# Four value groups at a time, and scores by key from the first maximum on, in a Perceiver's cross attentions

## The chip, the cores and the metric

The kernel runs as one program on one core of a Trainium2 chip. The metric is the device time of an execution in microseconds, lower is better; of several runs the median counts.

## The reference

Four layers work on a stream x of 256 tokens of width 256. Each layer has a cross attention from the stream to a context of 4,096 tokens, then an attention-like step among the 256 tokens and a feed-forward step. The change touches the cross attentions. Those of layers 2 and 3 are plain:

```python
qh = (q @ Wq.T + bq).reshape(B, Sq, H, HD).transpose(0, 2, 1, 3) / sqrt(HD)
kh = (k @ Wk.T + bk).reshape(B, Sk, H, HD).transpose(0, 2, 1, 3)
vh = (v @ Wv.T + bv).reshape(B, Sk, H, HD).transpose(0, 2, 1, 3)
scores = jnp.einsum('bhqd,bhkd->bhqk', qh, kh)
attn = jax.nn.softmax(scores, axis=-1)
ctx = jnp.einsum('bhqk,bhkd->bhqd', attn, vh)
```

with H = 16 heads of width 16, 256 queries (the normalised stream) and 4,096 keys. Layer 1 has a mask on the keys of each query; layer 0 has a mask too and multiplies the softmax by a given weight per query and key.

## The kernel before

The keys and values of all four layers are projected first. After that each layer runs `cross`, which puts three stages into one block: `queries`, `attend` and `project_out`. In `attend` every engine has its instruction list written out by a loop over the heads, and the engines meet at semaphores alone.

A head's scores are computed twice. **By query** (`by_queries`, L861): a chunk is 512 keys for 128 queries, one matmul into one bank of PSUM, and 16 chunks make a head. The vector engine only takes the maximum of each row of a chunk (L1070; with a mask L1066), and from 16 such columns the maximum of each query (`row_max`, L1075). GpSimd splits that maximum into three bf16 parts in four short steps (`split`, L1159 to L1162), the tensor engine turns it (`turn_max`, L931) and the scalar engine places it as three more rows of the queries' operand (`place_max`, L986), which signals max_set. **By key** (`by_keys`, L878; with a mask also L881): four key tiles of 128 keys by 256 queries, two banks, the maximum already subtracted by the three rows; 8 such groups make a head. The scalar engine exponentiates a group of 128 x 1024 (L1046) into one of eight buffers `prob`, and the tensor engine multiplies it with the values (`values`, L905, four matmuls of 32 columns each, side by side in the array), adding up in one bank. Values lag four groups behind. After a head's last group the scalar engine copies the sums (`read_sums`, L991), the tensor engine folds them (`fold`, L940) and the vector engine normalises (L1095, L1097).

The order of the tensor engine, and with it the steps of the scalar and the vector engine, is a string per head: C is a chunk by query, K a group by key, V two groups of values, T the turn of the next head's maximum, F the fold of the head before. In `PLAIN_ORDER` each head takes 16 C, 8 K and 4 V, and its C's run 24 chunks ahead: head h reduces the last 8 chunks of head h+1 and the first 8 of head h+2, so the turn T of head h+1 needs the eighth C of head h. The scalar engine places the maximum of head h+1 after the sixth group of head h (`TURN_AT`) and copies the sums of head h-1 after the fourth (`SUM_AT`).

Three limits tie the queues together. C and F share a ring of three banks: `ring_bank` waits until the reduction three uses ago is done. K has two pairs of banks: a group waits for the exponential two groups before. The exponential of group n waits until the values of group n-8 are done.

Ahead of the heads stands an opening of `FIRST` passes. A pass is two chunks into one of three pairs of banks, and the vector engine reduces 128 x 1024 at once. With `FIRST` = 12 the opening covers 24 chunks, that is head 0 and half of head 1; the maximum of head 0 is turned after pass 10 (`n == SC // 2 + 2`). In attention 1 GpSimd also prepares three groups of the mask (L1199, L1201) before it splits the first maximum.

```python
ORDER = WEIGHTED_ORDER if weighted else MASKED_ORDER if by_query else PLAIN_ORDER
i = slots.next()
if i >= RING:
    pe.wait_ge(S("s_read"), i - RING + 1)
```

Of the kernel before, what the change touches and what calls it, by code (L numbers as in the profile page):

```python
# [37 lines left out]
NGROUP = KT // GROUP  # L38
# [29 lines left out]

WEIGHTED_ORDER = "WK CCK C V C T C WK CCK C V F C WKK CCC V C KK W CCC V".replace(" ", "")
MASKED_ORDER = "CCK CCK CCK CVV CCK KCCKF CKCT KCCC VV".replace(" ", "")  # L70
PLAIN_ORDER = "CCKCKCCV CCKCKCV CKCCT KF CKCCKC VV".replace(" ", "")


class Sems:
# [695 lines left out]
def attend(c, l, by_query, weighted, ctx, asked, load_next):  # L770
# [3 lines left out]
    SC = QT * NCHUNK  # L774
    LAG = 2 if weighted else 4
    NP = 2 * LAG
    AHEAD = 32 if weighted else 24
    FIRST = AHEAD // 2
    ORDER = WEIGHTED_ORDER if weighted else MASKED_ORDER if by_query else PLAIN_ORDER
    SUM_AT, TURN_AT = (1, 1) if weighted else (2, 5) if by_query else (3, 5)  # L780
    SHIELD = (2, 5, 7) if l == SHIELDED else ()
    SHARED = (0, 2, 4, 6) if weighted else ()
    RING = 3
    ops, kop, qop, vraw = c.ops, c.ops.kop, c.qop, c.ops.vraw
    S = Sems(nc, ctx, f"att{l}")
    sb = lambda name, shape, dt: ctx.enter_context(nc.sbuf_tensor(f"{name}_a{l}", shape, dt))
# [22 lines left out]
    first_banks = [pair(0), pair(3), pair(5)]  # L809
    last_first = [max(n for n in range(FIRST) if n % 3 == r) for r in range(3)]  # L810
    st_order = sorted((1, 2), key=lambda r: last_first[r])
# [29 lines left out]
    def _(pe):  # L841
# [101 lines left out]

        for n in range(FIRST):
            if 2 * n % SC == 0:
                loaded(2 * n // SC)
            if n >= 3:
                pe.wait_ge(S("first_read"), n - 2)
            for i in range(2):
                ins = by_queries(first_banks[n % 3][:, i * CHUNK:(i + 1) * CHUNK], 2 * n + i)  # L950
            ins.then_inc(S("first_psum"), 1)
            if n == SC // 2 + 2:
                turn_max(0)

        for h in range(H):
            at, g, n = SC * h + AHEAD, 0, NGROUP * h - LAG
            for step in ORDER:
                if step == "C":
                    if at < SC * H:
                        if at % SC == 0:  # L960
                            loaded(at // SC)
                        by_queries(ring_bank(), at).then_inc(S("s_psum"), 1)
                    at += 1
                elif step == "K":
                    by_keys(h, g)
                    g += 1
                elif step == "V":
                    if n >= 0:
                        two_values(n)
                    n += 2  # L970
                elif step == "T" and h + 1 < H:
                    turn_max(h + 1)
                elif step == "F" and h > 0:
                    fold(h - 1)
# [6 lines left out]
    @stage.scalar  # L981
    def _(act):
        def place_max(h):

            act.wait_ge(S("max_turned"), h + 1)
            act.activation(qop[R_MAX:R_MASK, h, :], turn_out[R_MAX:R_MASK, :], ACT.Copy).then_inc(S("max_set"), 1)  # L986

        def read_sums(h):

            act.wait_ge(S("pv_psum"), NGROUP * (h + 1))  # L990
            act.activation(acc[:, h % 2, :], sums_out, ACT.Copy).then_inc(S("sums_read"), 1)  # L991

        if asked is None:
            act.activation(warm[:, :], c.ones[:, 0:1], ACT.Exp).then_inc(S("table"), 1)
        def sum_part(h, t, j, lowered, at):

            if h >= 4 and t == 0 and j == own[0]:
                act.wait_ge(S("gathered"), h - 3)
            act.activation(lowered, lowered, ACT.Exp, scale=-1.0, bias=best[:, h % 2, at:at + 1],  # L999
                           accum_out=part[:, h % 4, t, own.index(j):own.index(j) + 1]).then_inc(S("summed"), 1)  # L1000

        def find_scale(h):

            act.wait_ge(S("max_found"), h + 1)
            least = best[:, h % 2, :].rearrange("p (t j two) -> p t j two", t=QT, two=2)
            for t in range(QT):
                act.activation(scale[:, h % 4, t, :], least[:, t, :, 0 if h < 2 else 1], ACT.Exp, scale=-1.0,
                               bias=nmax[:, h % 2, t:t + 1]).then_inc(S("scaled"), 1)

        if weighted:  # L1010
            for n in range(FIRST):
                h, chunk = 2 * n // SC, 2 * n % SC
                act.wait_ge(S("first_read"), n + 1)
                sum_part(h, chunk // NCHUNK, chunk % NCHUNK + 1, used[:, n % NP, CHUNK:2 * CHUNK], chunk)
                if n == SC // 2 + 2:
                    find_scale(0)
                    place_max(0)
        else:
            place_max(0)
        slots, slot_of = Count(), {}  # L1020
        for h in range(H):
            at, g = SC * h + AHEAD, 0
            for step in ORDER:
                if step == "C":
                    last = at - 1
                    if last in slot_of and last % NCHUNK in own:
                        act.wait_ge(S("s_read"), slot_of[last] + 1)
                        hh, chunk = last // SC, last % SC
                        sum_part(hh, chunk // NCHUNK, chunk % NCHUNK, below[:, last // 2 % 2, :], chunk)
                    if at < SC * H:  # L1030
                        slot_of[at] = slots.next()
                    at += 1
                if step == "F" and h > 0:
                    slots.next()
                if step != "K":
                    continue
                n = NGROUP * h + g
                act.wait_ge(S("st_psum"), n + 1)
                if n >= NP:
                    act.wait_ge(S("pv_psum"), n - NP + 1)  # L1040
                if g in SHIELD:
                    act.activation(prob[:, n % NP, :], st_bank(n), ACT.Relu, scale=-1.0).then_inc(S("bounded"), 1)
                    act.wait_ge(S("bounded"), shields(n) + 1)
                    act.activation(prob[:, n % NP, :], prob[:, n % NP, :], ACT.Exp, scale=-1.0).then_inc(S("exp_done"), 1)  # L1044
                else:
                    act.activation(prob[:, n % NP, :], st_bank(n), ACT.Exp).then_inc(S("exp_done"), 1)  # L1046
                if g == SUM_AT and h > 0:
                    read_sums(h - 1)
                if g == SUM_AT and weighted and h + 1 < H:
                    find_scale(h + 1)  # L1050
                if g == TURN_AT and h + 1 < H:
                    place_max(h + 1)
                g += 1
        read_sums(H - 1)

    @stage.vector
    def _(dve):
# [45 lines left out]
        for n in range(FIRST):  # L1103
            h, chunk = 2 * n // SC, 2 * n % SC
# [9 lines left out]
                row_max(h)  # L1114
        dve.wait_ge(S("first_read"), FIRST)
        for h in range(H):
            at = SC * h + AHEAD
            for step in ORDER:
                if step == "C":
                    if at < SC * H:  # L1120
                        k = slots.next()
# [1639 lines left out]
```

## Time and profile before

| | us |
|---|---|
| median of three runs | 1492.37 |
| lowest and highest run | 1487.21, 1492.59 |
| the profiled execution | 1488.9 |
| its span, first to last instruction | 1487.5 |
| tensor engine, matmuls busy | 1356.0 (91% of the span) |
| vector engine busy | 1005.1 (68%) |
| scalar engine busy | 859.9 (58%) |
| GpSimd busy | 568.7 (38%) |
| mean granted clock of the tensor engine | 0.963 of full |

The heads of attention 1 lie from about 605 us on, those of attention 2 from 953 to 1153, those of attention 3 from 1242 to 1442. In a timeline a row is a run of like instructions on one engine: its start and length in microseconds, the engine, the line in the kernel, what it writes and reads, how many there are, and in brackets how long the engine was idle before and what ended that. The length of a matmul row reaches to the end of its last result, so rows overlap by the pipeline's depth, and costs are read from start to start. The matmuls of the values are recorded twice each (a row of x16 is two groups). PE is the tensor engine, DVE the vector engine, ACT the scalar engine, POOL GpSimd.

### The profile page before, as it was taken

The page shows a single profiled execution, that of the slowest core. Times are in us where ns is not written, and L with a number is a line of the kernel's source. Part 1 is how long each engine was busy: PE and PEld are TensorE (multiplying, and loading weights), DVE is VectorE, ACT ScalarE, POOL GpSimd, SP SyncE. Part 2 cuts the span into 40 slices and gives each one's busy share as a digit, 9 for nine tenths or more (in the row PEclk, how much of TensorE's full clock was granted, in tenths as well). Part 3 has the DMA queues.
Part 4 walks back from the last instruction along what each step waited for, and adds up shares of the span by engine and source line. Part 5 has one row for each costly group of instructions (what it writes and reads, how often), then busy time and mean ns, then how long its engine had stood idle before and what let it go on. Part 6 is the DMA issues. An engine that isn't in the chain of part 4 may idle for free. (4 is left out here: it accounts for less than half of the span.)

```text
span 1487.5 us, 28822 instructions
## 1 busy us (share of the span) xinstructions
PE 1356.0 (91%) x10423; PEld 802.3 (54%) x10496; DVE 1005.1 (68%) x2324; ACT 859.9 (58%) x1326; POOL 568.7 (38%) x686
## 2 busy tenths in 40 slices
PE   8999798999999988799999788699999896999987
PEld 3765656355555456355555554255555582555555
DVE  4445485999999734778787143588885337888832
ACT  5143141899999731388888552167777302777762
POOL 4565252688989920655555340111110001111100
PEclk9999999899999998899999999799999997999999
DMA  8877997246547053266655195257776711677700
GB/s 274 286 266 250 246 256 261 47 65 87 75 69 161 2 81 48 57 93 92 85 82 146 34 212 201 80 79 104 103 112 196 111 18 46 97 108 104 152 2 8
DMA packets 126008, 178.30 MB, mean 120 GB/s; under 512 B 14733, under 2 KB 106021, under 8 KB 116646
## 3 DMA queue, kind: packets, MB, share of 16 engines
q1 hardware_dynamic: 111898, 161.04, 52.9%
q10 hardware_dynamic: 13968, 15.41, 3.4%
q8 instruction: 84, 1.38, 0.4%
q14 instruction: 58, 0.48, 0.1%
HBM read 132.58 MB, written 43.78 MB: 119 GB/s over the span
## 5 line engine op out<-in xcount | busy, mean ns | idle before, releaser
L1046 ACT ACTIVATE prob_a<-ps 128x1024 f32<-128x1024 f32 x464 | 456.6, 1020 | 143.5 <-PE ps L878 95.4
L861 PE MATMUL ps<-kop,qop 116*128 116x512 bf16 x1024 | 345.4, 401 | 34.8 <-DMA qop<-qparts 21.8
L1070 DVE TENSOR_REDUCE best_a<-ps 128x1 f32<-128x512 f32 (+1 forms) x488 | 318.4, 709 | 49.4 <-PE ps L861 49.0
L878 PE MATMUL ps<-qop,kop 116*128 116x256 bf16 x2048 | 333.9, 274 | 7.7 <-ACT prob_a L1046 3.1
L878 PEld LDWEIGHTS ps<-qop,kop 116*128 116x128 bf16 x2048 | 193.8, 98 | 124.7 <-ACT prob_a L1046 21.9
L1066 DVE CUSTOM_DVE_ANT_0 dump_a<-ps,neg_q 128x512 bf16<-128x512 f32 (+1 forms) x244 | 165.9, 715 | 44.3 <-PE ps L861 42.2
L905 PE MATMUL ps<-prob_a,vop_a 128*32 128x256 f32 x3072 | 191.7, 383 | 3.1 <-POOL prob_a L1210 2.2
L861 PEld LDWEIGHTS ps<-kop,qop 116*128 116x128 bf16 x1024 | 95.2, 103 | 160.3 <-issue 64.3
L1180 POOL TENSOR_TENSOR used_a<-prob_a,gT 128x1024 f32<-128x1024 f32 x64 | 154.4, 2414 | 22.1 <-DVE used_a L1083 17.0
L1159 POOL CAST mpart_a<-nmax_a 128x2 bf16<-128x2 f32 x64 | 26.3, 411 | 348.1 <-DVE nmax_a L1075 348.1
L1210 POOL TENSOR_TENSOR prob_a<-prob_a,neg_k 128x1024 f32<-128x1024 f32 x48 | 102.5, 2135 | 92.8 <-ACT prob_a L1044 86.3
L905 PEld LDWEIGHTS ps<-prob_a,vop_a 128*32 128x32 f32 x3072 | 87.2, 109 | 82.6 <-issue 34.9
L503 PE MATMUL ps<-wv,ctxT 128*128 128x256 f32 x512 | 117.3, 392 | 14.4 <-DVE vst L648 14.4
L492 PE MATMUL ps<-ctxT,wk 128*128 128x512 f32 x256 | 112.6, 599 | 5.9 <-DMA wk<-in_wk 5.8
L503 PEld LDWEIGHTS ps<-wv,ctxT 128*128 128x128 f32 x512 | 100.5, 197 | 32.2 <-DVE vst L648 16.0
L538 ACT ACTIVATE kp<-ps,bk 128x512 bf16<-128x512 f32 x64 | 43.8, 686 | 127.8 <-PE ps L492 107.8
L1083 DVE SCALAR_TENSOR_TENSOR used_a<-prob_a,gT 128x1024 f32<-128x1024 f32 x64 | 95.5, 1492 | 9.0 <-ACT prob_a L1046 9.0
L668 POOL TENSOR_TENSOR kp<-rest,kp 128x512 bf16<-128x512 f32 x64 | 74.7, 1171 | 60.9 <-ACT kp L543 60.8
L211 POOL TENSOR_TENSOR rstd<-var,minus_half 128x2 f32<-128x2 f32 x11 | 7.8, 710 | 223.5 <-DVE var L201 215.6
L648 DVE TENSOR_TENSOR vst<-ps,bv 128x256 f32<-128x256 f32 x128 | 53.0, 423 | 59.4 <-PE ps L503 50.8
L881 PE MATMUL ps<-neg_k,identb 128*128 128x512 bf16 x225 | 86.2, 383 | 0.0
L999 ACT ACTIVATE below_a<-below_a,best_a 128x512 f32<-128x512 f32 x112 | 80.3, 717 | 9.2 <-DVE best_a L1062 8.6
(333 smaller groups left out, 1768.0 us busy)
## 6 DMA issues: line engine op xcount, KB each, us to landing
kop<-kparts SPq DMA_DIRECT2D x448, 128.0 KB, 5.2
kparts<-kp SPq DMA_DIRECT2D x64, 384.0 KB, 4.7
vals<-vst SPq DMA_DIRECT2D x16, 1024.0 KB, 5.2
vraw<-vals SPq DMA_DIRECT2D x64, 256.0 KB, 6.6
e_w<-in_e_w SPq DMA_DIRECT2D x4, 2048.0 KB, 10.8
z_w<-in_z_w SPq DMA_DIRECT2D x24, 256.0 KB, 7.0
ctxT<-in_ctxT SPq DMA_DIRECT2D x8, 512.0 KB, 8.0
raw<-in_mask ACTq DMA_DIRECT2D x16, 256.0 KB, 5.3
```

Of the source, the lines that this page charges most:

```text
L492: ins = pe.matmul(c.ps[:, K_BANKS[u % 4], :], wk[:, ct, mt * P:(mt + 1) * P], ctxT[:, ct, j * CHUNK:(j + 1) * CHUNK], start=(ct == 0), sto ...
L503: ins = pe.matmul(c.ps[:, V_BANKS[v % 4], 0:D], ctxT[:, ct, k * P:(k + 1) * P], wv[:, ct, :], start=(ct == 0), stop=(ct == CT - 1))
L861: return pe.matmul(out, qop[0:R_ALL, h, t * P:(t + 1) * P], kop[0:R_ALL, h % UNROLL, j * CHUNK:(j + 1) * CHUNK], start=True, stop=True)
L878: ins = pe.matmul(st_bank(n)[:, j * NT:(j + 1) * NT], kop[0:R_ALL, h % UNROLL, k * P:(k + 1) * P], qop[0:R_ALL, h, :], start=(j % 2 == 0), ...
L881: ins = pe.matmul(st_bank(n)[:, (j - 1) * NT:(j + 1) * NT], c.identb[:, :], c.neg_k[:, k - 1:k + 1, :], start=False, stop=True)
L905: ins = pe.matmul(sums_out[32 * j:32 * j + 32, :], vop[:, h % 2, g * GROUP + j, :], used[:, n % NP, j * NT:(j + 1) * NT], start=(g == 0 an ...
L1046: act.activation(prob[:, n % NP, :], st_bank(n), ACT.Exp).then_inc(S("exp_done"), 1)
L1066: dve.tensor_tensor_reduce(out=dump[:, k % 2, 0:width], in0=bank, in1=c.neg_q[:, t, j * CHUNK:j * CHUNK + width], scale=1.0, scalar=-3.0e3 ...
L1070: dve.tensor_reduce(out, bank, AX.X, ALU.max).then_inc(sem, 1)
L1083: dve.scalar_tensor_tensor(out=used[:, n % NP, :], in0=prob[:, n % NP, :], scalar=1.0, in1=c.gT[:, g * GROUP:(g + 1) * GROUP, :].rearrange ...
L1180: pool.tensor_tensor(used[:, n % NP, :], prob[:, n % NP, :], c.gT[:, g * GROUP:(g + 1) * GROUP, :].rearrange("p k q -> p (k q)"), ALU.mult)\
L1210: pool.tensor_tensor(prob[:, n % NP, :], prob[:, n % NP, :], seen(g).rearrange("p k q -> p (k q)"), ALU.mult)\
```

## The change

It has two parts. In the two plain attentions a head's values stand in two blocks of four groups; before, there were two blocks of two groups and one of four. Number and order of the C, K, T and F steps among each other stay. In the last three attentions (1, 2 and 3) the opening has 8 passes, not 12, and head 0 has an order of its own, `OPENING_ORDER`, with 24 C and a step M for the turn of the first maximum. Attention 1 keeps `MASKED_ORDER` for its other heads, attention 0 is unchanged.

```diff
--- before.py
+++ after.py
@@ -68,7 +68,8 @@
 
 WEIGHTED_ORDER = "WK CCK C V C T C WK CCK C V F C WKK CCC V C KK W CCC V".replace(" ", "")
 MASKED_ORDER = "CCK CCK CCK CVV CCK KCCKF CKCT KCCC VV".replace(" ", "")
-PLAIN_ORDER = "CCKCKCCV CCKCKCV CKCCT KF CKCCKC VV".replace(" ", "")
+PLAIN_ORDER = "CCKCKCC CCKCKC VV CKCCT KF CKCCKC VV".replace(" ", "")
+OPENING_ORDER = "CCCM CKCCKCCKCCKCCC VV CCKC T CK CFK CCCK CCC VV".replace(" ", "")
 
 
 class Sems:
@@ -775,12 +776,14 @@
     LAG = 2 if weighted else 4
     NP = 2 * LAG
     AHEAD = 32 if weighted else 24
-    FIRST = AHEAD // 2
+    FIRST = (AHEAD if weighted else SC) // 2
     ORDER = WEIGHTED_ORDER if weighted else MASKED_ORDER if by_query else PLAIN_ORDER
     SUM_AT, TURN_AT = (1, 1) if weighted else (2, 5) if by_query else (3, 5)
     SHIELD = (2, 5, 7) if l == SHIELDED else ()
     SHARED = (0, 2, 4, 6) if weighted else ()
     RING = 3
+    order = lambda h: OPENING_ORDER if h == 0 and not weighted else ORDER
+    chunks_from = lambda h: 2 * FIRST if h == 0 else SC * h + AHEAD
     ops, kop, qop, vraw = c.ops, c.ops.kop, c.qop, c.ops.vraw
     S = Sems(nc, ctx, f"att{l}")
     sb = lambda name, shape, dt: ctx.enter_context(nc.sbuf_tensor(f"{name}_a{l}", shape, dt))
@@ -949,12 +952,12 @@
             for i in range(2):
                 ins = by_queries(first_banks[n % 3][:, i * CHUNK:(i + 1) * CHUNK], 2 * n + i)
             ins.then_inc(S("first_psum"), 1)
-            if n == SC // 2 + 2:
+            if weighted and n == SC // 2 + 2:
                 turn_max(0)
 
         for h in range(H):
-            at, g, n = SC * h + AHEAD, 0, NGROUP * h - LAG
-            for step in ORDER:
+            at, g, n = chunks_from(h), 0, NGROUP * h - LAG
+            for step in order(h):
                 if step == "C":
                     if at < SC * H:
                         if at % SC == 0:
@@ -968,6 +971,8 @@
                     if n >= 0:
                         two_values(n)
                     n += 2
+                elif step == "M":
+                    turn_max(0)
                 elif step == "T" and h + 1 < H:
                     turn_max(h + 1)
                 elif step == "F" and h > 0:
@@ -1019,8 +1024,8 @@
             place_max(0)
         slots, slot_of = Count(), {}
         for h in range(H):
-            at, g = SC * h + AHEAD, 0
-            for step in ORDER:
+            at, g = chunks_from(h), 0
+            for step in order(h):
                 if step == "C":
                     last = at - 1
                     if last in slot_of and last % NCHUNK in own:
@@ -1114,8 +1119,8 @@
                 row_max(h)
         dve.wait_ge(S("first_read"), FIRST)
         for h in range(H):
-            at = SC * h + AHEAD
-            for step in ORDER:
+            at = chunks_from(h)
+            for step in order(h):
                 if step == "C":
                     if at < SC * H:
                         k = slots.next()
```

The tensor engine's queue in head 1 of attention 2, from the end of head 0's only block of values on. Here 512-wide rows are C (L861), x4 of 256 are K (L878), and 32x256 are values (L905). Before:

```order
L861 MATMUL ps<-kop,qop 128x512 x2
L878 MATMUL ps<-qop,kop 128x256 x4
L861 MATMUL ps<-kop,qop 128x512
L878 MATMUL ps<-qop,kop 128x256 x4
L861 MATMUL ps<-kop,qop 128x512 x2
L905 MATMUL ps<-prob_a,vop_a 32x256 x8
L861 MATMUL ps<-kop,qop 128x512 x2
L878 MATMUL ps<-qop,kop 128x256 x4
L861 MATMUL ps<-kop,qop 128x512
L878 MATMUL ps<-qop,kop 128x256 x4
L861 MATMUL ps<-kop,qop 128x512
L905 MATMUL ps<-prob_a,vop_a 32x256 x8
```

With the change (the lines are three further down, L864, L881, L908):

```order
L864 MATMUL ps<-kop,qop 128x512 x2
L881 MATMUL ps<-qop,kop 128x256 x4
L864 MATMUL ps<-kop,qop 128x512
L881 MATMUL ps<-qop,kop 128x256 x4
L864 MATMUL ps<-kop,qop 128x512 x4
L881 MATMUL ps<-qop,kop 128x256 x4
L864 MATMUL ps<-kop,qop 128x512
L881 MATMUL ps<-qop,kop 128x256 x4
L864 MATMUL ps<-kop,qop 128x512
L908 MATMUL ps<-prob_a,vop_a 32x256 x16
```

The block of eight value matmuls after the fifth C is gone, so that four C's stand together, and the second block has sixteen.

The same queue at the start of attention 2, from the first pass on; L931 (later L934) is the turn of a maximum. Before:

```order
L861 MATMUL ps<-kop,qop 128x512 x22
L931 MATMUL ps<-identb,mpart_a 99x128 x2
L861 MATMUL ps<-kop,qop 128x512 x4
L878 MATMUL ps<-qop,kop 128x256 x4
L861 MATMUL ps<-kop,qop 128x512
L878 MATMUL ps<-qop,kop 128x256 x4
L861 MATMUL ps<-kop,qop 128x512 x4
```

With the change:

```order
L864 MATMUL ps<-kop,qop 128x512 x19
L934 MATMUL ps<-identb,mpart_a 99x128 x2
L864 MATMUL ps<-kop,qop 128x512
L881 MATMUL ps<-qop,kop 128x256 x4
L864 MATMUL ps<-kop,qop 128x512 x2
L881 MATMUL ps<-qop,kop 128x256 x4
L864 MATMUL ps<-kop,qop 128x512 x2
L881 MATMUL ps<-qop,kop 128x256 x4
```

The first turn stands after 19 chunks, not 22, and one chunk, not four, stands between it and the first scores by key.

The same queue around the turn of head 1's maximum, in head 0 of attention 2. Before:

```order
L878 MATMUL ps<-qop,kop 128x256 x4
L861 MATMUL ps<-kop,qop 128x512
L878 MATMUL ps<-qop,kop 128x256 x4
L861 MATMUL ps<-kop,qop 128x512 x2
L878 MATMUL ps<-qop,kop 128x256 x4
L861 MATMUL ps<-kop,qop 128x512 x2
L931 MATMUL ps<-identb,mpart_a 99x128 x2
L878 MATMUL ps<-qop,kop 128x256 x4
L861 MATMUL ps<-kop,qop 128x512
```

With the change:

```order
L864 MATMUL ps<-kop,qop 128x512 x5
L881 MATMUL ps<-qop,kop 128x256 x4
L864 MATMUL ps<-kop,qop 128x512
L934 MATMUL ps<-identb,mpart_a 99x128 x2
L864 MATMUL ps<-kop,qop 128x512
L881 MATMUL ps<-qop,kop 128x256 x4
L864 MATMUL ps<-kop,qop 128x512
L881 MATMUL ps<-qop,kop 128x256 x4
```

Before, head 1's last chunk, 31, is the second row here, and the chunks 32 to 35 and two groups by key stand between it and the turn. Now chunk 31 is the single chunk right ahead of the turn.

## Rows read from the trace of the kernel before

**Rows 1.** Busy time by engine over the steady heads of attentions 2 and 3 (stretches).
```profile
979.30:1130.80 151.50, 151.50 (x1539) 87.55 (x1536) 134.29 (x247) 111.11 (x130) 17.31 (x65) 1.00 0.79 130
1267.80:1419.00 151.20, 151.20 (x1537) 87.42 (x1534) 134.32 (x247) 111.11 (x130) 17.30 (x65) 1.00 0.71 112
```

**Rows 2.** Timeline of the tensor engine, head 1 of attention 2 (start us, us, engine, line).
```profile
979.31 0.60 PE L861 MATMUL ps<-kop,qop 116*128 116x512 bf16 x2
...
980.18 0.38 PE L861 MATMUL ps<-kop,qop 116*128 116x512 bf16 x1
980.40 0.60 PE L878 MATMUL ps<-qop,kop 116*128 116x256 bf16 x4
980.84 0.63 PE L861 MATMUL ps<-kop,qop 116*128 116x512 bf16 x2
981.40 1.07 PE L905 MATMUL ps<-prob_a,vop_a 128*32 128x256 f32 x16
982.40 0.60 PE L861 MATMUL ps<-kop,qop 116*128 116x512 bf16 x2
...
990.96 0.61 PE L861 MATMUL ps<-kop,qop 116*128 116x512 bf16 x2
```

**Rows 3.** Timeline of the vector engine, head 1 of attention 2.
```profile
979.73 4.98 DVE L1070 TENSOR_REDUCE best_a<-ps 128x1 f32<-128x512 f32 x8 [1.35 <-PE ps L861]
...
987.83 2.48 DVE L1070 TENSOR_REDUCE best_a<-ps 128x1 f32<-128x512 f32 x4
```

**Rows 4.** Timeline of the tensor engine, heads 14 and 15 of attention 2.
```profile
1137.51 0.32 PE L931 MATMUL ps<-identb,mpart_a 128*99 128x128 bf16 x2 [0.41 <-POOL mpart_a L1162]
...
1141.79 1.05 PE L878 MATMUL ps<-qop,kop 116*128 116x256 bf16 x8
```

**Rows 5.** Timeline of the scalar engine, head 15 of attention 2.
```profile
1142.44 3.92 ACT L1046 ACTIVATE prob_a<-ps 128x1024 f32<-128x1024 f32 x4 [0.74 <-PE ps L878]
...
1146.62 3.77 ACT L1046 ACTIVATE prob_a<-ps 128x1024 f32<-128x1024 f32 x4
```

**Rows 6.** Timeline of the tensor engine, opening of attention 2.
```profile
965.11 0.45 PE L931 MATMUL ps<-identb,mpart_a 128*99 128x128 bf16 x2 [0.25 <-POOL mpart_a L1162]
...
967.42 1.03 PE L878 MATMUL ps<-qop,kop 116*128 116x256 bf16 x4
...
977.44 1.93 PE L905 MATMUL ps<-prob_a,vop_a 128*32 128x256 f32 x32
```

**Rows 7.** Timeline of the vector engine, opening of attention 2.
```profile
963.80 0.17 DVE L1075 TENSOR_REDUCE nmax_a<-best_a 128x2 f32<-128x16 f32 x1
963.89 9.51 DVE L1070 TENSOR_REDUCE best_a<-ps 128x1 f32<-128x1024 f32 x12
...
973.52 4.86 DVE L1070 TENSOR_REDUCE best_a<-ps 128x1 f32<-128x512 f32 x8
```

**Rows 8.** Timeline of the scalar engine, opening of attention 2.
```profile
965.60 0.38 ACT L986 ACTIVATE qop<-ps 3x256 bf16<-3x256 f32 x1 [18.79 <-PE ps L931]
```

**Rows 9.** Stretches of the openings: tensor engine's busy time (count) and granted clock.
```profile
957.90:961.20 3.30, 1.95 (x7) 1.00 0.00 0
968.10:971.40 3.30, 3.30 (x11) 0.50 0.01 2
1254.90:1258.10 3.20, 3.10 (x13) 0.50 0.00 0
1258.30:1261.60 3.30, 2.79 (x15) 1.00 0.00 0
```

**Rows 10.** Timeline of the tensor engine, opening of attention 3.
```profile
1258.99 0.39 PE L861 MATMUL ps<-kop,qop 116*128 116x512 bf16 x1 [0.21 <-DVE best_a L1070]
1259.59 0.39 PE L861 MATMUL ps<-kop,qop 116*128 116x512 bf16 x1 [0.21 <-DVE best_a L1070]
...
1265.88 1.93 PE L905 MATMUL ps<-prob_a,vop_a 128*32 128x256 f32 x32
```

**Rows 11.** Timeline of the tensor engine, opening of attention 1.
```profile
617.29 0.45 PE L931 MATMUL ps<-identb,mpart_a 128*99 128x128 bf16 x2 [0.68 <-POOL mpart_a L1162]
```

## The prediction

> **What bounds the kernel now.** I read the changed stages one at a time. First the busy time of each engine over the steady heads of the two plain attentions: the tensor engine is busy for all of 151.50 us and all of 151.20 us, the vector engine for 134.3 us, the scalar engine for 111.1 us [rows 1]. So the tensor queue's order is the bound there, and the vector engine has some 11% to spare, on average. The average is not enough: the vector engine frees the three banks of the ring, so where the order puts many C steps together the ring decides. For that I read the tensor engine's timeline of head 1 of attention 2 [rows 2] beside the vector engine's [rows 3]. Then the two last heads [rows 4, 5], and the opening, where the vector engine is the bound: it reduces without a gap from 963.89 to 978.38 us [rows 7], while the tensor engine starts its first block of values at 977.44 [rows 6]. I call 512 scores by query a C, a group of scores by key a K, and two groups of values a V.
>
> **Prices.** From starts in [rows 2]: a C 0.22 us (980.18 to the K at 980.40), a K 0.44 (980.40 to 980.84). A block of two groups lasts 1.00 (981.40 to 982.40), one of four 1.87 (977.44 [rows 6] to 979.31). So a group costs 0.87/2 = 0.435 and 0.13 of each block belongs to no group. Ahead of the block at 981.40 two C's take 0.56, not 0.44; 0.03 of that is a ring wait (their row lasts 0.63, those of other pairs 0.60 or 0.61), 0.09 is the block's entry. **A block saved gives 0.22 us.** A reduction of 512 on the vector engine goes at 0.61 us (4.86 [rows 7] and 4.98 us for eight, 2.48 for four) and begins 0.42 us after its C does (979.31, 979.73) [rows 2, 3].
>
> **The plain heads, part by part.** Removed: one block per head in heads 1 to 15, that is 30 blocks, 30 x 0.22 = 6.6 us. Moved: the first V goes behind the second, so that the tensor queue holds two C's, a K, a C, a K and then four C's in a row, where the V stood after the second of the four. A C may start when the reduction of the third C before it is done. In the trace's time for head 1: the reductions end at 979.73 + 0.61 n. The sixth C would start at 981.28 without waiting, but needs the third reduction, over at 981.56, plus about 0.1 for the signal: 981.65. The seventh needs the fourth: 982.26, and would have started at about 981.50. **That is 0.76 us of stall**; the fifth C already waits 0.03 in the trace, the ring's edge showing. And the pattern is in the trace once: in head 0 no values are due yet, so there four C's do stand in a row, and in attention 3 at full clock the third and the fourth of them start at 1258.99 and 1259.59, 0.60 apart and each held back by a reduction [rows 10]. The eighth and ninth C come after a K each and need 982.88 and 983.49; the queue brings them at 982.92 and 983.58. So a head gains 0.22, loses 0.76, and is longer by 0.54 us. The values hide none of it, since the block now stands behind the stall; during its 1.87 us the vector engine drains the ring (at most three reductions, 1.83 us) and then idles.
>
> Heads 1 to 13: 13 x 0.54 = 7.0 us. Head 14 has eight C's, all ahead of its first block: +0.54, but its turn of the maximum waited 0.41 for the GpSimd split [rows 4] and now has a longer block ahead of it: +0.1. Head 15 has no C's; the exponentials set its pace, at 0.92 us (four in 3.77, the last lasting 1.02) [rows 5]. Its K's begin at 1141.79; the third may start when the first exponential is over (1143.4), the fourth after the second (1144.3), ends at 1144.8; the block of four ends at 1146.8, and the fifth K's exponential starts at 1147.4 where it stood at 1146.62 [rows 4, 5]: +0.8. One plain attention: 7.0 + 0.1 + 0.8 = 7.9; two: **+15.8 us**. The sums of the previous head are read later (its last values are in the moved block), but before the fifth K's exponential, so the scalar engine's 27% of idle time takes that; the turn of the next maximum has more slack than before.
>
> **The openings** (attentions 1, 2, 3). Four passes of two chunks and four of 1024-wide reductions become eight single C's and eight reductions of 512. In attention 2 the first maximum is turned at 965.11 as before [rows 6]: it waits for the row maximum at 963.80 and four GpSimd steps, 1.31 us in all [rows 6, 7]. The scalar engine has placed it at 965.98 [rows 8], so the first K starts at about 966.1, not 967.42. But the vector engine was not idle in between, and the tensor engine's clock is at half until 971.4 [rows 9], where I take a C at 0.44 and a K at 0.87. After the first K come (two C's, a K) three times: K done 966.9, C's 967.8, K 968.7, C's 969.6, K 970.4, C's 971.3, K 971.8. The vector engine gets two chunks in each 1.75 us, uses 1.22, and idles. It reaches the six chunks that are left of head 1 at 972.2 and has done them at 975.9. **Now the turn of head 1's maximum stands directly behind its last chunk**: row maximum, split and signal, 1.31 us, so the turn is at 977.2 and the next C at 977.3; before, four C's and two K's stood in between. The last eight C's go at the vector engine's pace: reductions from 977.75, the fifth over at 980.8, the last C at 980.9, the block of values at 981.2. Before: 977.44. **+3.8 us.** Attention 3 has full clock from 1258.2 [rows 9]: the same steps give reductions without a gap from 1257.85, ten of them to 1263.95, the turn at 1265.25, the block 4.0 later at 1269.25, before 1265.88 [rows 10]: +3.4. Attention 1 has the same order, slightly longer reductions, two more matmuls of mask in most K's, and its maximum turned at 617.29 because of the row maximum and split, not the shields' preparation [rows 11]; I take the mean of the other two, 3.6. Sum **+10.8 us**. After the opening the tensor engine is the bound without a gap [rows 1], so nothing is caught up later. No DMA is moved: the loads for head 4 wait for head 0's eighth K, a few us later, with three heads of slack.
>
> Bounds of an opening, which the trace cannot show: below, if the clock were full from 965 on, only the idle time at the turn is left (975.9 to 977.75, 1.85 us), which I round down to 1.5 us each since a little of it lies under the tensor engine's own work. Above, if the stall at the turn brings the clock back to half for the eight C's and the block after it, the 3.1 us from the turn and the 1.87 us block double in part: 7 us each. I take the middle by the rows. For a steady head the ends are 0.45 and 0.60 (reduction at 0.60 or 0.625), so 14 to 18 us for both attentions.
>
> The Trainium skill, page "TensorEngine Tiling", section "Key Properties", says that changing the tiling mode drains the tensor engine; the 0.22 us per block in [rows 2] agrees. By that rule alone the change would be a gain; this is rival A below. The Trainium skill, page "TensorEngine Tiling", section "PSUM Bottleneck", says that emptying PSUM may become the bottleneck once the matmuls are faster; the 0.03 us wait at the fifth C agrees, and what I forecast is this rule deciding between two blocks though not over a whole head.
>
> **Sum.** 15.8 + 10.8 = +26.6 us. The profiled execution took 1488.9 us (span 1487.5), so it would be 1515.5; the median of the three runs, 1492.4, is 3.5 above it and they spread over 5.4 us. Predicted median: **1519 us**.
>
> **The rivals.** About 0.5% (7.5 us) is what a measurement of this kernel can tell from no change.
> A, faster: the ring does not stall the four C's, only the blocks are saved (-6.6), and the K's that start 1.3 us earlier carry through in the three openings (-3.9): 1482. It decides if the vector engine frees a bank in 0.42 us or less ((981.5 - 0.1 - 979.73)/4). For it: full use of the tensor engine and 11% slack on the vector engine [rows 1]. Against it: the eight reductions in 4.98 us [rows 3], the fifth C's 0.03 and the two waits in [rows 10]. Chance 0.05.
> B, no change: the heads gain 6.6, the openings cost 10.8: +4, 1496.5. It needs the ring to keep up in heads and not in openings. 0.05.
> C: the heads cost 15.8, the openings nothing, or gain 3.9 in part, because the clock stays at full once scores by key begin early: +12 to +16, 1504 to 1508. For it: only clock and placing of one turn make the loss. Against: the wait at the turn does not depend on the clock. 0.12.
> D: the clock falls to half behind the turn in some of the openings: +5 to +10 on the forecast, 1524 to 1530. For it: in attention 2 the clock was lowered while the tensor engine waited for the vector engine [rows 9]. 0.13.
> The forecast itself: 0.65.
>
> **How the numbers follow.** The forecast with its bounds reaches from 1492.4 + 14 + 4.5 = 1511 to 1492.4 + 18 + 21 = 1531; C takes the lower end to 1504, D stays inside; 1 us more at each end for the runs' spread. A and B, 0.10, are left out. Slower by over 0.5%: forecast, C and D, 0.90; same 0.05; faster 0.05.
>
> **What would show it.** In a plain head: four C's in a row whose last two are each 0.35 to 0.4 us late on a reduction, one four-group block with 1.87 us after them, and 12.2 us from head to head (now 990.96 - 979.31 = 11.65). In the openings: the first K about 1.3 us earlier, a wait of 2.5 us and more for the GpSimd split ahead of the second turn, vector engine idle nearly 2 us there, the first block of values 3 to 4 us later. If the head's period is 11.4 us, the ring did not bind and A or B holds. If the clock is at half behind the second turn, D. What would make me wrong in the terms: the opening's clock, above all.

## The result, and the profile after

The changed kernel takes 1522.27 us (median of four runs, 1517.96 to 1524.07), against 1490.51 for the kernel before on the same chip (four runs, 1487.21 to 1492.59): a ratio of 1.0193, 95% interval 1.0164 to 1.0222. It is slower by 1.9%. The profiled execution took 1521.92 us (span 1520.7), that of before 1488.9 (span 1487.5).

The page of the changed kernel, the engines' busy time, and of its costliest groups the matmuls of the chunks and the reductions (here and in the rows below, `...` marks rows left out):

```profile
PE 1369.4 (90%) x10496; PEld 810.6 (53%) x10496; DVE 1005.7 (66%) x2340; ACT 861.3 (57%) x1326; POOL 568.7 (37%) x686
...
L864 PE MATMUL ps<-kop,qop 116*128 116x512 bf16 x1024 | 350.6, 402 | 48.7 <-DMA qop<-qparts 20.7
L1075 DVE TENSOR_REDUCE best_a<-ps 128x1 f32<-128x512 f32 (+1 forms) x496 | 317.6, 700 | 72.7 <-PE ps L864 72.7
```

The reductions on the page of the kernel before:

```profile
L1070 DVE TENSOR_REDUCE best_a<-ps 128x1 f32<-128x512 f32 (+1 forms) x488 | 318.4, 709 | 49.4 <-PE ps L861 49.0
```

The work is the same: the scalar engine was busy for 861 us, before 860, the vector engine for 1006, before 1005. The tensor engine was busy for 13 us more, while the span grew by 33. A part of these 13 us are records (10,423 matmuls stood in the trace before, all 10,496 now); the rest was not traced. What grew is waiting: the vector engine sat idle for 72.7 us ahead of the reductions (L1075), before 49.4. The steady heads of attention 2, beside [rows 1]:

```profile
993.40:1150.90 157.50, 152.09 (x1530) 88.22 (x1530) 133.10 (x247) 111.33 (x130) 18.12 (x65) 1.00 0.75 125
```

Before, no microsecond of such a stretch was idle on the tensor engine; now 5.4 of 157.5 are. The tensor engine's timeline of one head (beside [rows 2]; columns are start, length, engine, line):

```profile
993.38 0.61 PE L864 MATMUL ps<-kop,qop 116*128 116x512 bf16 x2
...
994.25 0.38 PE L864 MATMUL ps<-kop,qop 116*128 116x512 bf16 x1
...
994.91 0.63 PE L864 MATMUL ps<-kop,qop 116*128 116x512 bf16 x2
995.75 0.39 PE L864 MATMUL ps<-kop,qop 116*128 116x512 bf16 x1 [0.21 <-DVE best_a L1075]
996.35 0.39 PE L864 MATMUL ps<-kop,qop 116*128 116x512 bf16 x1 [0.21 <-DVE best_a L1075]
...
997.97 1.93 PE L908 MATMUL ps<-prob_a,vop_a 128*32 128x256 f32 x32
999.84 0.39 PE L864 MATMUL ps<-kop,qop 116*128 116x512 bf16 x1
...
1005.55 0.61 PE L864 MATMUL ps<-kop,qop 116*128 116x512 bf16 x2
```

The vector engine's timeline of the same head (beside [rows 3]):

```profile
993.80 4.88 DVE L1075 TENSOR_REDUCE best_a<-ps 128x1 f32<-128x512 f32 x8 [0.79 <-PE ps L864]
...
1000.26 1.94 DVE L1075 TENSOR_REDUCE best_a<-ps 128x1 f32<-128x512 f32 x3 [0.78 <-PE ps L864]
```

On the tensor engine the row at 994.91 holds the first two of the four chunks, the next two stand alone, 0.60 us apart, each held back by a reduction. The last starts at 996.35, and without waiting would at 994.91 + 3 x 0.22 = 995.57. From head to head it is 1005.55 - 993.38 = 12.17 us, where it was 11.65. The vector engine reduces eight chunks in 4.88 us without a gap, and then idles in the long block (0.78 us before 1000.26). The same holds for all the steady heads: the mean over eleven of them, from fold to fold, is 12.172 in attention 2 and 12.173 in attention 3, before 11.650 in both.

The opening of attention 2, timeline of the tensor engine (beside [rows 6]):

```profile
962.70 4.40 PE L864 MATMUL ps<-kop,qop 116*128 116x512 bf16 x10 [7.63 <-DMA qop<-qparts]
...
974.30 0.45 PE L934 MATMUL ps<-identb,mpart_a 128*99 128x128 bf16 x2 [1.51 <-POOL mpart_a L1167]
...
975.31 1.01 PE L881 MATMUL ps<-qop,kop 116*128 116x256 bf16 x4
...
980.86 1.08 PE L864 MATMUL ps<-kop,qop 116*128 116x512 bf16 x3
982.14 0.39 PE L864 MATMUL ps<-kop,qop 116*128 116x512 bf16 x1 [0.21 <-DVE best_a L1075]
982.74 0.39 PE L864 MATMUL ps<-kop,qop 116*128 116x512 bf16 x1 [0.21 <-DVE best_a L1075]
...
983.40 0.38 PE L864 MATMUL ps<-kop,qop 116*128 116x512 bf16 x1
986.48 0.32 PE L934 MATMUL ps<-identb,mpart_a 128*99 128x128 bf16 x2 [2.70 <-POOL mpart_a L1167]
...
987.72 1.06 PE L881 MATMUL ps<-qop,kop 116*128 116x256 bf16 x4
...
991.51 1.93 PE L908 MATMUL ps<-prob_a,vop_a 128*32 128x256 f32 x32
```

The same opening on the vector engine (beside [rows 7]):

```profile
973.00 0.17 DVE L1080 TENSOR_REDUCE nmax_a<-best_a 128x2 f32<-128x16 f32 x1
973.09 1.88 DVE L1075 TENSOR_REDUCE best_a<-ps 128x1 f32<-128x512 f32 x3
975.22 0.69 DVE L1075 TENSOR_REDUCE best_a<-ps 128x1 f32<-128x512 f32 x1 [0.25 <-PE ps L864]
976.79 1.29 DVE L1075 TENSOR_REDUCE best_a<-ps 128x1 f32<-128x512 f32 x2 [0.88 <-PE ps L864]
978.49 1.29 DVE L1075 TENSOR_REDUCE best_a<-ps 128x1 f32<-128x512 f32 x2 [0.42 <-PE ps L864]
980.20 4.88 DVE L1075 TENSOR_REDUCE best_a<-ps 128x1 f32<-128x512 f32 x8 [0.42 <-PE ps L864]
985.11 0.17 DVE L1080 TENSOR_REDUCE nmax_a<-best_a 128x2 f32<-128x16 f32 x1
987.05 0.69 DVE L1075 TENSOR_REDUCE best_a<-ps 128x1 f32<-128x512 f32 x1 [1.77 <-PE ps L864]
```

Stretches around the second turn of attention 2 and behind those of attentions 1 and 3 (beside [rows 9]; stretch, length, tensor engine busy (count), granted clock):

```profile
983.80:987.10 3.30, 0.62 (x6) 1.00 0.00 0
987.20:990.50 3.30, 3.30 (x15) 0.51 0.00 0
990.60:993.30 2.70, 2.70 (x37) 0.98 0.57 121
632.30:635.50 3.20, 3.20 (x13) 0.50 0.00 0
1287.60:1290.90 3.30, 3.30 (x14) 0.51 0.00 0
```

The first scores by key follow the first turn by 1.01 us, where it was 2.31. The vector engine is idle for 0.25, 0.88, 0.42 and 0.42 us while groups by key go through at half clock (1.06 for a row of four, against 0.60), and 1.77 us at the second turn; the tensor engine waits 2.70 us there, with 0.62 us of work between 983.8 and 987.1, and from about 987.2 to 990.5 its granted clock is at half (1.2 GHz). Behind the second turns of attentions 1 and 3, at 631.05 and 1287.30, it is at half for some 3 us as well. The first block of values starts 991.51 - 962.70 = 28.81 us after the first pass, was 977.44 - 953.50 = 23.94.

Where the 33.2 us of span went, from the starts of the first pass, of the first block of values and of the last block, in both profiles:

| stretch | before | after | more |
|---|---|---|---|
| start to the first pass of attention 1 | 605.54 | 607.14 | 1.60 |
| opening of attention 1 | 25.96 | 29.40 | 3.44 |
| from there to the first pass of attention 2 | 322.00 | 326.16 | 4.16 |
| opening of attention 2 | 23.94 | 28.81 | 4.87 |
| heads of attention 2 | 171.71 | 179.63 | 7.92 |
| from there to the first pass of attention 3 | 92.88 | 92.56 | -0.32 |
| opening of attention 3 | 23.85 | 29.05 | 5.20 |
| heads of attention 3 | 171.72 | 179.63 | 7.91 |
| last block of values to the end | 49.9 | 48.3 | -1.6 |

Openings 13.5, heads 15.8, and 3.9 in stretches that the change does not touch. The largest of those, 4.16, contains the heads of attention 1 (13.574 us each, as before) and the steps behind it. The seven experiments below leave that stretch alone too, and needed 322.8 to 326.0 us for it, so the profiled execution of before was the quickest of nine there and that of the change the slowest. The table's 33.2 us hold some luck of this kind; the 29.3 us of openings and heads are what the change shows.

### The profile page after: what moved, and what is told of

The parts are those of the page before. It is cut to its first block and busy times, and to the rows that moved or that the text cites. A ratio compares the mean times of both kernels' runs of the same rounds, so it can differ in the third digit from the quotient of the medians.

```text
span 1520.7 us, 28915 instructions
## 1 busy us (share of the span) xinstructions
PE 1369.4 (90%) x10496; PEld 810.6 (53%) x10496; DVE 1005.7 (66%) x2340; ACT 861.3 (57%) x1326; POOL 568.7 (37%) x686
## 5 line engine op out<-in xcount | busy, mean ns | idle before, releaser
L864 PE MATMUL ps<-kop,qop 116*128 116x512 bf16 x1024 | 350.6, 402 | 48.7 <-DMA qop<-qparts 20.7
L1075 DVE TENSOR_REDUCE best_a<-ps 128x1 f32<-128x512 f32 (+1 forms) x496 | 317.6, 700 | 72.7 <-PE ps L864 72.7
L881 PE MATMUL ps<-qop,kop 116*128 116x256 bf16 x2048 | 337.4, 277 | 5.0 <-ACT prob_a L1051 4.5
L881 PEld LDWEIGHTS ps<-qop,kop 116*128 116x128 bf16 x2048 | 196.2, 99 | 124.2 <-ACT prob_a L1051 20.9
L864 PEld LDWEIGHTS ps<-kop,qop 116*128 116x128 bf16 x1024 | 99.0, 104 | 176.9 <-DVE best_a L1075 60.6
L908 PE MATMUL ps<-prob_a,vop_a 128*32 128x256 f32 x3072 | 185.5, 382 | 3.1 <-POOL prob_a L1215 2.2
L1215 POOL TENSOR_TENSOR prob_a<-prob_a,neg_k 128x1024 f32<-128x1024 f32 x48 | 102.5, 2134 | 94.9 <-ACT prob_a L1049 90.4
L908 PEld LDWEIGHTS ps<-prob_a,vop_a 128*32 128x32 f32 x3072 | 90.4, 110 | 79.4 <-issue 26.8
L884 PE MATMUL ps<-neg_k,identb 128*128 128x512 bf16 x288 | 111.2, 386 | 0.0
## 6 DMA issues: line engine op xcount, KB each, us to landing
e_w<-in_e_w SPq DMA_DIRECT2D x4, 2048.0 KB, 10.7
```

The costliest lines, as they stand in the source:

```text
L864: return pe.matmul(out, qop[0:R_ALL, h, t * P:(t + 1) * P], kop[0:R_ALL, h % UNROLL, j * CHUNK:(j + 1) * CHUNK], start=True, stop=True)
L881: ins = pe.matmul(st_bank(n)[:, j * NT:(j + 1) * NT], kop[0:R_ALL, h % UNROLL, k * P:(k + 1) * P], qop[0:R_ALL, h, :], start=(j % 2 == 0), ...
L884: ins = pe.matmul(st_bank(n)[:, (j - 1) * NT:(j + 1) * NT], c.identb[:, :], c.neg_k[:, k - 1:k + 1, :], start=False, stop=True)
L908: ins = pe.matmul(sums_out[32 * j:32 * j + 32, :], vop[:, h % 2, g * GROUP + j, :], used[:, n % NP, j * NT:(j + 1) * NT], start=(g == 0 an ...
L1075: dve.tensor_reduce(out, bank, AX.X, ALU.max).then_inc(sem, 1)
L1215: pool.tensor_tensor(prob[:, n % NP, :], prob[:, n % NP, :], seen(g).rearrange("p k q -> p (k q)"), ALU.mult)\
```

## The experiments

The two parts alone, first.

**The heads alone**: the kernel before with the new order.

```diff
-PLAIN_ORDER = "CCKCKCCV CCKCKCV CKCCT KF CKCCKC VV".replace(" ", "")
+PLAIN_ORDER = "CCKCKCC CCKCKC VV CKCCT KF CKCCKC VV".replace(" ", "")
```

> The new order of the plain heads, with the opening of before. My theory (the third and fourth of four chunks in a row wait for the ring of three banks, 0.76 us a head, against 0.22 us for the block saved): 12.19 us from head to head in attentions 2 and 3, 7.9 us more from the first block of values to the last in each, 15.8 us more in all, ratio 1.0106. Rival (the heads are slower only because the new opening leaves the queues in another phase): 11.43 to 11.65 us from head to head, 0 to 7 us less in all.

Measured: 1507.9 against 1493.4, ratio 1.0121 (1.0082 to 1.0161), 14.5 us by the medians. From head to head 12.172 us in both attentions, first to last block of values 7.9 us more in each, and the openings of both as before (23.94 and 23.87). The rival (another phase of the queues) fails. The heads' part is a property of their order.

**The openings alone**: the changed kernel with the old `PLAIN_ORDER` (the same diff backwards).

> The new openings, with the old order of the plain heads. From the changed kernel's trace, first pass to first block of values: 3.4 us more in attention 1, 4.9 in 2, 5.2 in 3, together 13.5 us, and 11.65 us from head to head; ratio 1.009. Rival (the opening costs only together with the new order, or part of it is caught up in the heads): under 1.004.

Measured: 1505.2 against 1493.4, ratio 1.0100 (1.0063 to 1.0137). First pass to first block of values: 31.22 us in attention 1 (5.3 more), 29.14 in 2 (5.2), 29.03 in 3 (5.2), together 15.6, where 13.5 was expected; the heads behind them 11.65. Nothing is caught up. The 2.1 us above the expectation are nearly all in attention 1, and the traces show where: the granted clock is back at full 17.9 us after the first pass here (half from 611.1 to 620.5), and 14.9 us in the profile of the change (half from 615.6 to 621.8), and the second turn stands 25.2 us behind the first pass here and 23.9 there. The same opening before the change took 25.2 to 26.1 us in attention 1 over five profiles, so a difference of two profiles is uncertain by about 1 us there. The two parts add to 26.3 us by medians (14.5 and 11.8), 31.4 by the traces (15.8 and 15.6); the change itself is at 31.8, and the intervals of the ratios allow that.

**Is it the run of four chunks or the long block?** One kernel has the run but no long block more, the other long blocks but no run; openings of before.

```diff
-PLAIN_ORDER = "CCKCKCCV CCKCKCV CKCCT KF CKCCKC VV".replace(" ", "")
+PLAIN_ORDER = "CCKCKCC CCKCV K CV CKCCT KF CKCCKC VV".replace(" ", "")
```

> Opening of before, and in the plain heads three blocks as before, but the first two groups of values moved behind four chunks in a row, with one group by key between the two blocks of two groups. So no block is saved and the run of four is there. Theory of the ring: 0.76 us longer per head, 12.4 us from head to head, 11 us more in each of attentions 2 and 3, 22 in all, more than the change's own 15.8. Rival (what costs is the long block): 11.65, nothing.

Measured: 1515.0 against 1492.7, ratio 1.0144 (1.0116 to 1.0172); 12.416 us from head to head, 0.766 more than before; 11.1 us more in each attention. The rows of the tensor engine in attention 2, with the run between 1061.81 and 1063.24:

```profile
1061.81 0.63 PE L861 MATMUL ps<-kop,qop 116*128 116x512 bf16 x2
1062.65 0.39 PE L861 MATMUL ps<-kop,qop 116*128 116x512 bf16 x1 [0.21 <-DVE best_a L1070]
1063.24 0.39 PE L861 MATMUL ps<-kop,qop 116*128 116x512 bf16 x1 [0.21 <-DVE best_a L1070]
```

The forecast stall was 0.76. Against the heads alone this kernel has the same run and one block more per head, and differs by 12.416 - 12.172 = 0.244 us: the price of a block, forecast at 0.22.

```diff
-PLAIN_ORDER = "CCKCKCCV CCKCKCV CKCCT KF CKCCKC VV".replace(" ", "")
+PLAIN_ORDER = "CCKCK CCKCCKC VV CCKCT KFCK CCKCC VV".replace(" ", "")
```

> Two blocks of four groups per plain head as in the change, but no run of more than two chunks without scores by key between them; opening of before. Theory of the ring: the long block still drains the ring and eight chunks stand between two blocks, so a little waiting stays, about 11.95 us from head to head, 4.3 us more in each of attentions 2 and 3, 8.6 in all. Rival (the long block itself is what costs, whatever stands around it): 12.19 us from head to head, 15.8 in all. Rival (only the run of four costs): 11.43, about 5 us less.

Measured: 1500.7 against 1493.4, ratio 1.0061 (1.0040 to 1.0082); 11.865 us from head to head (expected about 11.95), first to last block 3.5 us more in each attention, and 0.6 in the openings, whose first head has this order too. Both rivals fall: the long block is not what costs, and breaking up the run is not enough to keep the block's gain. With the block saved and no waiting it would be 11.650 - 0.244 = 11.41 (the price of a block is that of the kernel above), so 0.46 us of waiting are left. Two rows of the tensor engine hold 0.27 of it by the starts behind them, the pair of chunks at 1055.49 that lasts 0.76 and not 0.60, and the one at 1050.37 with 0.72:

```profile
1050.37 0.72 PE L861 MATMUL ps<-kop,qop 116*128 116x512 bf16 x2
...
1055.49 0.76 PE L861 MATMUL ps<-kop,qop 116*128 116x512 bf16 x2
```

The other 0.18 is not the ring. The group by key at 1055.04 follows its pair of chunks (1054.42) after 0.62 us and not 0.44, and the timeline of the weight loads says what it waits for, the scalar engine's exponential two groups before:

```profile
1055.04 0.33 PEld L878 LDWEIGHTS ps<-qop,kop 116*128 116x128 bf16 x4 [0.29 <-ACT prob_a L1046]
```

**What the run waits for.** Attention 2 has the new order, attention 3 the old one, and the single chunks of both are reduced over half their columns (so the maximum is over half of the later keys).

```diff
+JOINED_ORDER = "CCKCKCC CCKCKC VV CKCCT KF CKCCKC VV".replace(" ", "")
-    ORDER = WEIGHTED_ORDER if weighted else MASKED_ORDER if by_query else PLAIN_ORDER
+    ORDER = WEIGHTED_ORDER if weighted else MASKED_ORDER if by_query else JOINED_ORDER if l == KEYED else PLAIN_ORDER
-                        chunk_max(best[:, at // SC % 2, chunk:chunk + 1], c.ps[:, k % RING, :], chunk // NCHUNK,
+                        chunk_max(best[:, at // SC % 2, chunk:chunk + 1],
+                                  c.ps[:, k % RING, :] if by_query else c.ps[:, k % RING, 0:CHUNK // 2], chunk // NCHUNK,
```

> Attention 2 has the new order, attention 3 the old one, opening of before, and in the heads of both the vector engine reduces 256 of the 512 columns of a chunk, so that the maximum is over half of the later keys. Theory of the ring: with reductions of about 0.35 us no chunk waits for a bank, and what is left is the block saved: 11.43 us from head to head in attention 2, 11.65 in attention 3. Rival (the wait is for something else than the reduction's length, the signal or the bank): attention 2 stays over 11.9.

Measured, in a single run: 11.633 us from head to head with the new order, 11.614 with the old one. So the half-wide reduction takes the new order from 12.172 to 11.633 and the old one only from 11.650 to 11.614 (the fifth chunk's 0.03). The rival (over 11.9) fails, but 11.43 was forecast for the new one, and it is not there. The run of four shows why. The tensor engine in a head of attention 2:

```profile
1042.69 1.29 PE L862 MATMUL ps<-kop,qop 116*128 116x512 bf16 x4
1043.82 0.60 PE L879 MATMUL ps<-qop,kop 116*128 116x256 bf16 x4
```

And its reductions:

```profile
1041.59 1.29 DVE L1071 TENSOR_REDUCE best_a<-ps 128x1 f32<-128x256 f32 x3 [1.76 <-PE ps L862]
1043.11 1.99 DVE L1071 TENSOR_REDUCE best_a<-ps 128x1 f32<-128x256 f32 x5 [0.23 <-PE ps L862]
```

The run takes 1043.82 - 1042.69 = 1.13 us, some 0.26 more than four chunks at 0.22. The reduction of the run's first chunk starts 0.42 us after the chunk, and the trace records 0.42 us for a reduction of this width (they follow one another at some 0.34). So the bank is not back until over 0.84 us after the chunk began, while three chunks take 0.66; the fourth starts at about 1043.82 - 0.22 = 1043.60, 0.91 after the first. It waits for the first one's bank even where the vector engine is not behind. 11.614 - 0.244 + 0.26 = 11.63 is what was measured. So 0.50 of the 0.76 us go when the reductions are half as wide, and 0.26 stay: one chunk's way through the vector engine, wait, short reduction and signal together.

**The openings.** Both of these kernels have the old order in the heads.

```diff
-OPENING_ORDER = "CCCM CKCCKCCKCCKCCC VV CCKC T CK CFK CCCK CCC VV".replace(" ", "")
+OPENING_ORDER = "CCCM CKCCKCCKCCKCCC VV CCKCCKCCC T K CC K CC VV".replace(" ", "")
```

> Old order of the plain heads, new openings with one thing moved: the turn of head 1's maximum stands four chunks and one group by key after head 1's last chunk, no longer directly behind it (the groups after it close up). Theory (about half of the opening's loss is the idle time at this turn): the wait at the turn falls from 2.7 us to under 0.5, the first block of values is 2.7 to 3.3 us after where it stands in before in attentions 2 and 3, not 5.2, and the median is about 6 us under that of the openings alone. Rival (the vector engine is the bound in the whole opening, the turn only shows it): still 4.5 us or more per attention.

Measured: 1499.1 against 1492.7, ratio 1.0040 (1.0025 to 1.0055), 6.1 us under the openings alone by the medians. First pass to first block of values: 27.41, 25.31 and 25.96 us in attentions 1, 2 and 3, that is 1.5, 1.4 and 2.1 more than before; together 4.9, not 15.6. The gain is larger than expected (2.7 to 3.3 us more were forecast for attentions 2 and 3), and the rival (4.5 us or more) fails. The opening of attention 2 around that turn:

```profile
980.70 0.38 PE L864 MATMUL ps<-kop,qop 116*128 116x512 bf16 x1 [0.24 <-DVE best_a L1075]
...
981.35 0.85 PE L864 MATMUL ps<-kop,qop 116*128 116x512 bf16 x2
982.61 0.39 PE L864 MATMUL ps<-kop,qop 116*128 116x512 bf16 x1 [0.41 <-DVE best_a L1075]
983.16 0.32 PE L934 MATMUL ps<-identb,mpart_a 128*99 128x128 bf16 x2 [0.16 <-POOL mpart_a L1167]
...
985.32 1.93 PE L908 MATMUL ps<-prob_a,vop_a 128*32 128x256 f32 x32
```

The clock behind it:

```profile
983.00:987.00 4.00, 3.84 (x46) 1.00 0.26 72
```

The turn at 983.16 waits 0.16 us, and the clock is full from 983 to 987; behind the second turns of attentions 1 and 3 (634.68 and 1274.60) it is full for the next 4 us as well. The openings gained 10.7 us, more than the 7.6 us of the three waits at the turn (2.23, 2.70, 2.62): with the wait the half clock behind it is gone too.

```diff
-OPENING_ORDER = "CCCM CKCCKCCKCCKCCC VV CCKC T CK CFK CCCK CCC VV".replace(" ", "")
+OPENING_ORDER = "CCCCCCM CC CCKCKCC CCKCKC CKCCT K CKCCKC VVVV".replace(" ", "")
```

> Old order of the plain heads, opening of 8 passes, then a first head whose steps stand in exactly the tensor queue's order of before: the last 4 passes of two chunks are eight single chunks through the ring of three banks, reduced 512 wide. It tells what the single chunks cost by themselves. Theory: 8 x 0.61 - 4 x 1.137 = 0.3 us of reduction and 0.7 us because the first turn comes behind three chunks more of the ring: the first block of values 1.0 to 1.5 us later per attention, at most 2.4 if the clock falls differently; 3 to 5 us in all. Rival (three banks instead of six take the lead that the tensor engine needs, and that is the opening's loss): 4 us or more per attention.

Measured: 1497.9 against 1492.7, ratio 1.0040 (1.0022 to 1.0059). The first block of values is 0.9 and 0.6 us later than before in attentions 2 and 3 (expected 1.0 to 1.5), and the rival (4 us or more) fails. The single chunks by themselves cost that much, the rest of the 5.2 is the order. In attention 1 it is 3.1, over the bound of 2.4 that I had set; there this order is not the one of before (its head 0 had the masked one), and the turn stands where GpSimd is busy with another thing:

```profile
631.03 2.13 POOL L1215 TENSOR_TENSOR prob_a<-prob_a,neg_k 128x1024 f32<-128x1024 f32 x1 [7.63 <-issue]
633.11 0.19 POOL L1164 CAST mpart_a<-nmax_a 128x2 bf16<-128x2 f32 x1
...
633.91 0.20 POOL L1167 TENSOR_TENSOR mpart_a<-mrest_a,mpart_a 128x2 bf16<-128x2 f32 x1
```

The mask of the third group (L1215, 2.13 us) goes ahead of the split in GpSimd's queue, and the split ends at 634.1; the turn had waited 2.56 us for it. The clock behind this turn, stretch on the tensor engine:

```profile
634.20:640.00 5.80, 5.33 (x56) 1.00 0.40 75
```

It stays full, though the wait was as long as those of the change, behind which it fell. So the half clock goes with the wait at this turn in the change's opening, but the length of the wait alone does not decide it.

None of these versions beats the kernel before.

## Why the prediction was right

The forecast was 1519 us, range 1503 to 1532, slower with 0.90; it is 1522.3, and by difference +26.6 against +31.8. The heads came out as forecast for the forecast's reason; in the openings a term was too small. Against the kernel before as measured on other occasions (medians 1493.4 and 1492.7, on two chips) the difference would be 28.9 and 29.6, near the 29.3 us of the stretches that the change touches.

- **The stall in a run of four.** Forecast 0.76 us by the reductions' pace: the run alone makes a head 0.766 longer. The step that carried it was the trace of head 0 in [rows 10], where a run of four was already there.
- **The block saved.** Forecast 0.22: 0.244 between two kernels that differ in it. The drain between tiling modes, which the Trainium skill names in "TensorEngine Tiling", section "Key Properties", may be the reason; the runs agree with a price of that size for a block, and do not separate the drain from what else a block costs. Rival A, which had only gains, failed at 12.17 us a head.
- **The heads.** Forecast 0.54 a head and 7.9 an attention: 0.522, and 7.92 and 7.91. Head 15 was forecast 0.8 longer up to its fifth exponential: from its first group by key that is 1168.60 - 1162.91 = 5.69 us after, 1146.62 - 1141.79 = 4.83 before, so 0.86.
- **The openings, the term that was too small.** Forecast 3.8, 3.4 and 3.6 us for attentions 2, 3 and 1: measured 4.87, 5.20 and 3.44, with the openings alone 5.2, 5.2 and 5.3. The mechanism was right up to the second turn: it stands 23.8 and 23.6 us behind the first pass in attentions 2 and 3, forecast 23.7 and 23.2. (The 0.4 us in attention 3 come from reductions that were to run without a gap from 15.8 us after the first pass, and did from 17.4.) What failed is the last step, "the last eight C's go at the vector engine's pace": from the turn to the block it took 5.0 and 5.5 us, not 4.0, because the clock was at half for some 3 us behind the turn, in all three attentions (5.5 us in attention 1 too). That is rival D, which I had made a case of its own with +5 to +10 us; it happened everywhere, but was short, 1 to 1.5 us each. That attention 1 came out at 3.44 beside a forecast of 3.6 is luck: the clock was back at full 3 us earlier there than in the other profile of the same opening, which took 5.3 us more, and this made up for the half clock behind the turn. What sets the clock there was not tried.
- **Rival C** (openings that cost nothing) failed; B failed with A.
- **Why the ring stalls.** The prediction's sum already held the 0.42 us ahead of a reduction and 0.1 behind it, so its 0.76 was right, but the price at which it said the stall is gone, "in 0.42 us or less" per reduction, is not what the half-wide reductions showed: at some 0.34 us each the run still waits 0.26. That bound counted the seventh chunk from the head's first reduction on, as if the vector engine never ran dry; with short reductions it does, before the run, and the way there and back counts anew.

The profiled execution was forecast at 1515.5 and took 1521.9. Of the 33.2 us of its span 29.3 lie in the changed stretches, 2.7 above the forecast, and 3.9 in stretches that the change does not touch; no term of the forecast stands for these.

## What to carry to other kernels

Before work is joined to save the cost of switching, look at what the pieces were keeping apart: here each block of values was the time in which the vector engine emptied three banks, and taking one out for 0.24 us put four chunks in a row, which cost 0.77. The engine with 11% to spare over a head was the bound inside the run, since three banks cover neither its pace nor the way to it and back. And a step that waits for the end of a chain (reduce, split over a third engine, turn) belongs some work behind the chain's start: moved next to it, it cost 2.2 to 2.7 us of waiting, and here the clock was at half for some 3 us after.

## What the runs showed of the hardware

- The run of four matmuls into a ring of three banks takes 0.26 us too long even where a reduction is recorded with only 0.42 us; 0.42 us pass between a matmul's start and the reduction's.
- A block of column-tiled fp32 matmuls between bf16 ones costs 0.244 us beside its matmuls here, the difference per head between two kernels with the same run of chunks and two or three blocks.
- At a wait of 2.2 to 2.7 us at the second turn the granted clock fell to half (1.2 GHz) in all three openings of the change, and in all three of the openings alone, and was full again some 3 us later; with the turn moved, where it waited 0.16 us or less, it stayed full in all three. It also stayed full behind a wait of 2.56 us, in attention 1 with the old steps. The same opening cost attention 1 3.4 us in one profile and 5.3 in the other.
